# Second step of a two-layer graph kernel: norm statistics of four rows in two groups, and the top-eight pass between reading the flags and loading their register

## Chip, cores and metric

The kernel runs on one core of a Trainium2 chip. The metric is the device time of one launch in microseconds (us), lower is better: the median of three runs before the change is 4236.88 us (4235.11 to 4237.03).

## What is computed

Layer 0 is a graph attention over 4096 nodes with a dense 0/1 adjacency, residual and layer norm. Layer 1, cut to what matters here, is

```
for n in range(2):
    A  = top_p(softmax((Xa@W1.T@W2.T) @ (Xa@W3.T).T), 0.9)   # 4096 x 4096, rows renormalised
    Xf = R @ Xf                                               # R = (adj + I) / row sums
    Xa = A @ Xa
    Z  = Z + Xf @ U1[n].T + Xa @ U2[n].T
h = layernorm(X + Z) * ln_g + ln_b
out = layernorm(X + h)
```

`top_p` keeps, in each row, the smallest set of largest probabilities whose sum reaches 0.9. The layer norm is `(h - mean) / sqrt(var + 1e-5)`.

## The kernel before

The five engines run programs written out by hand and meet only through semaphores. Layer 0 comes first, then two steps `s = 0` and `s = 1` of layer 1. The change is in the second step (`s == 1`), which begins near 2400 us. It works through 32 tiles n of 128 rows each, with a score row of 4096 per partition, in three score buffers.

**VectorE**, per tile t: `search(t)` waits for the exponentials (`xp`) and for three halvings that ScalarE has already made (`lt`), makes three full passes over the scores (L1265), calls `final_stats(t)`, makes a fourth full pass (L1271), takes the top eight of 16 chunks (L1277), and sorts 48 candidates (L1284, L1286). `threshold(t)` (L1297 to L1325) works out the cut in some twenty small instructions and signals `lv`. `finish(t)` marks ties (L1333, L1334), calls `rmax(t + 2)`, waits for the row of flags that TensorE has turned (`pl`), reduces it to one integer (L1381), loads that integer into a register (L1382), branches on it (L1383; the branch's body is hardly ever run), and writes the masked scores (L1392), which signals `mask`. `rmax(t)` is one top-eight pass over 4096 scores (L1212) and a negation of the largest (L1213), which signals `mx`. In this code `link(ins)` lets the engine's next instruction wait until `ins` has completed.

`final_stats(n)` makes the mean and variance of rows of 128 x 256 for the two closing layer norms. Slots of two row tiles each enter the pipe from tile n = 17 on (`fslot`). For each of up to four row tiles (two that wait for `f1`, two that wait for `fa`) `stats_of` runs four instructions: `bn_stats` (L1232), `bn_aggr` (L1233), the negated mean (L1234) and variance plus epsilon (L1235), then signals `s2` or `s1`. Three of the four are linked. It is called with two row tiles at n = 18, with four at n = 19 to 31, and after the last tile in the loop's own extra rounds n = 32 to 36.

**GpSimd**, per round n: `r_post` (L529 to L537) ends the rows of R, `final_second`, `final_first` and `final_add` do the norms of three different slots (`norm` is L543 to L545), `scale_a` (L509 to L515) and `accumulate` (L523) end a tile of A @ Xa, and `bracket(n + 2)` (L484 to L503) prepares the search of tile n + 2. It starts when ScalarE signals `e8`, and its L492 signals `bt`.

**ScalarE**, per round n: evicts the turned scores, the logits of tile n + 3 (L958) and small products, runs three halvings of tile n + 1 (L1012 waits for `bt`; L1013, L1014 are full passes), evicts row 2p of R (L1043), runs `expo(n + 2)` (L994 waits for `mx`, L1002 ends with `e8`) and evicts row 2p + 1.

**TensorE**, per round n: `Tr(n - 1)` (L804) waits for `mask`, then logits (L760), small products, `AV(n - 1)` (L815), `Rmul(2p)` (L719), `gather_level(n)` (L821, waits for `lv`), `Rmul(2p + 1)` (L719). Rows r = 2p of R run up to 64: 32 for the first product, then 32 for the second, which reads `y_d` back into SBUF at n = 15.

**SyncE** loads the adjacency chunks, and stores and reloads `y_d`, `h_d`, `z_d` and `out`, in one queue in program order.

Of the kernel before, what the change touches and what calls it, by code (L numbers as in the profile page):

```python
# [9 lines left out]
ALU = mybir.AluOpType  # L10
# [7 lines left out]
EPS = 1e-5  # L18
# [8 lines left out]
def gat_topp_kernel(nc, xT, x, adj, adjTb, Wp, WT, aT, res_w, bias, res_b, ident, sel,  # L27
                    W1, W2T, W3T, U1T, U2T, ln_g, ln_b, out):
    N = adj.shape[0]
    NT = N // 128  # L30
# [19 lines left out]
    fslot = {max(HT + m - RLEAD + 2, 2 * m + 4): m for m in range(HT)}  # L50
# [10 lines left out]
    with ctx:  # L61
# [18 lines left out]
        def bank(b, n=1):  # L80
            return ps[:, 512 * b:512 * (b + n)]

        def sem(name):
            return ctx.enter_context(nc.semaphore(name))
# [70 lines left out]
        e8 = r1.take(8)  # L155
# [8 lines left out]
        m8 = r1.take(2, 8)  # L164
# [24 lines left out]
        fin = r1.take(6, 256)  # L189
        finx = r1.take(4, 256)  # L190
        finz = r1.take(2, 256)
        lns = r1.take(4, 16)
# [13 lines left out]
        def scores(s, t):  # L206
            return eb[:, t % (2 + s), 0:N]
# [70 lines left out]
        for s in range(2):  # L278
            g = {}
            for n in ("kt", "kc", "km", "kk", "pl", "el", "mx", "xp", "mask", "av", "R", "rv", "pz", "gx",  # L280
                      "gd", "po", "rd", "xs", "acc", "nz", "hi", "gi", "yd", "ys", "fi", "fa", "s1", "f1", "s2",
                      "fo", "fd", "lv", "lr", "lt", "qd", "e8", "bt", "bf", "xc"):
                g[n] = sem(f"{n}_{s}")
            g["aj"] = [sem(f"aj{i}_{s}") for i in range(AJR)]
            g["xd"] = [sem(f"xd{i}_{s}") for i in range(2)]
            st.append(g)
# [158 lines left out]
        def _(po):  # L445
# [13 lines left out]
            for i in range(16):  # L459
                last = nc.gpsimd.memset(iota[:, i:i + 1], float(i))  # L460
# [4 lines left out]
            def plink(ins):  # L465
                pc[0] += 1
                ins.then_inc(s_pc, 1)
                po.wait_ge(s_pc, pc[0])

            tt = nc.gpsimd.tensor_tensor  # L470
            ts = nc.gpsimd.tensor_scalar
            for s in range(2):
                g = st[s]
# [66 lines left out]
                def norm(r, dst, sem_):  # L540
                    a = lns[:, r % 4, :]
                    po.wait_ge(sem_, r + 1)
                    plink(tt(a[:, 8:9], a[:, 6:7], mhalf, ALU.pow))  # L543
                    plink(tt(a[:, 9:10], a[:, 8:9], a[:, 7:8], ALU.mult))
                    return ts(dst, fin[:, r % 6, :], a[:, 8:9], a[:, 9:10], ALU.mult, ALU.add)  # L545

                def final_add(m):
                    po.wait_ge(g["fi"], 16 * 6 * (m + 1))
# [4 lines left out]
                def final_first(m):  # L553
                    for r in (2 * m, 2 * m + 1):
                        f = fin[:, r % 6, :]
                        plink(norm(r, f, g["s1"]))
                        plink(tt(f, f, gb[:, 0, :], ALU.mult))
                        plink(tt(f, f, gb[:, 1, :], ALU.add))
                        tt(f, f, finx[:, r % 4, :], ALU.add).then_inc(g["f1"], 1)

                def final_second(m):
                    for r in (2 * m, 2 * m + 1):
                        norm(r, fin[:, r % 6, :], g["s2"]).then_inc(g["fo"], 1)
# [547 lines left out]
        def _(ve):  # L1111
            v = nc.vector

            def link(ins):
                dvc[0] += 1
                ins.then_inc(s_dv, 1)
                ve.wait_ge(s_dv, dvc[0])

            def done(sm_):
                ve.sem_inc(sm_, 1)  # L1120
# [7 lines left out]
            dst = WA[:, :, 256:264].rearrange("p k (h e) -> p k h e", e=2)[:, :, :, 1]  # L1128
            v.tensor_copy(WD[:, :, 0:4], dst)
            last = v.tensor_copy(WD[:, :, 32:36], dst)  # L1130
# [69 lines left out]
            def inner(ins):  # L1200
                ins.then_inc(s_br, 1)
                ve.wait_ge(s_br, 1)
                ve.sem_clear(s_br)

            for s in range(2):
                g = st[s]
                theta, mid, G, tmp, hi, ghi, t_, c8, r_, nt_, lo, nota, x_, y_ = (sm[:, 2 + i:3 + i] for i in range(14))
                cut, part, rl, rr = (sm[:, 16 + i:17 + i] for i in range(4))

                def rmax(t):  # L1210
                    ve.wait_ge(g["el"], eat[t])
                    link(v.max(m8[:, t % 2, :], scores(s, t)))  # L1212
                    v.tensor_scalar(sm[:, t % 2:t % 2 + 1], m8[:, t % 2, 0:1], -1.0, None,  # L1213
                                    ALU.mult).then_inc(g["mx"], 1)

                def cmax(t):
                    E = scores(s, t)
                    CK = N // NCHUNK[0]
                    for c in range(NL // 2):
                        ve.wait_ge(g["el"], eat[t] - NL // 2 + 1 + c)  # L1220
                        for lo_ in (c * 512, N // 2 + c * 512):
                            for k in range(lo_ // CK, (lo_ + 512) // CK):
                                last = v.max(cand[:, t % 2, k * 8:k * 8 + 8], E[:, k * CK:(k + 1) * CK])
                    link(last)
                    top = cand[:, t % 2, :].rearrange("p (c e) -> p c e", e=8)[:, :, 0]
                    link(v.tensor_reduce(m8[:, t % 2, 0:1], top, AX.X, ALU.max))
                    v.tensor_scalar(sm[:, t % 2:t % 2 + 1], m8[:, t % 2, 0:1], -1.0, None,
                                    ALU.mult).then_inc(g["mx"], 1)

                def stats_of(r, sem_):  # L1230
                    a = lns[:, r % 4, :]
                    link(v.bn_stats(a[:, 0:6], fin[:, r % 6, :]))  # L1232
                    link(v.bn_aggr(a[:, 10:12], a[:, 0:6]))  # L1233
                    v.tensor_scalar(a[:, 7:8], a[:, 10:11], -1.0, None, ALU.mult)  # L1234
                    link(v.tensor_scalar(a[:, 6:7], a[:, 11:12], EPS, None, ALU.add))  # L1235
                    done(sem_)

                def final_stats(n):
                    if s == 1 and n - 2 in fslot:
                        for r in (2 * fslot[n - 2], 2 * fslot[n - 2] + 1):  # L1240
                            ve.wait_ge(g["f1"], r + 1)
                            stats_of(r, g["s2"])
                    if s == 1 and n - 1 in fslot:
                        for r in (2 * fslot[n - 1], 2 * fslot[n - 1] + 1):
                            ve.wait_ge(g["fa"], r + 1)
                            stats_of(r, g["s1"])

                def search(t):
                    E = scores(s, t)
# [77 lines left out]
                def mark(sync, t, j):  # L1327
                    io = iota[:, 8 * j:8 * j + 8]
                    v.tensor_scalar(w8[:, 0, :], io, rl, t_, ALU.is_lt, ALU.mult)
                    sync(v.tensor_scalar(w8[:, 1, :], io, rr, t_, ALU.is_lt, ALU.mult))  # L1330
                    src = scores(s, t) if j == 0 else V
                    HN = N // 2
                    v.match_replace(out=V[:, 0:HN], in_to_replace=w8[:, 0, :], in_values=src[:, 0:HN], imm_value=2.0)  # L1333
                    sync(v.match_replace(out=V[:, HN:N], in_to_replace=w8[:, 1, :], in_values=src[:, HN:N],  # L1334
                                         imm_value=2.0))
# [32 lines left out]
                def finish(t):  # L1368
                    E = scores(s, t)
                    VN = V[:, 0:N]  # L1370
                    if s == 1:
                        mark(link, t, 0)
                        if t + 2 < NT:
                            rmax(t + 2)
                    if s == 0:
                        ve.wait_ge(g["lr"], t + 1)
                        flags = levr[0:1, :]
                    else:
                        ve.wait_ge(g["pl"], levat[t])
                        flags = bank(2 * ((levat[t] - 1) % 3))[0:1, 0:128]  # L1380
                    link(v.tensor_reduce(levi[0:1, :], flags, AX.X, ALU.max))  # L1381
                    level = ve.value_load(levi[0:1, :], min_val=0, max_val=2)  # L1382
                    with ve.If(level >= 1):  # L1383
                        if s == 0:
                            mark(inner, t, 0)
                        mark(inner, t, 1)
                        with ve.If(level >= 2):
                            exact(E)
                        if s == 0:
                            inner(v.scalar_tensor_tensor(out=E, in0=VN, scalar=t_, in1=E, op0=ALU.is_gt,  # L1390
                                                         op1=ALU.mult))
                    v.scalar_tensor_tensor(out=E, in0=VN if s else E, scalar=cut if s else t_, in1=E,  # L1392
                                           op0=ALU.is_gt if s else ALU.is_ge, op1=ALU.mult).then_inc(g["mask"], 1)
# [17 lines left out]
                if s == 0:  # L1411
                    cmax(0)
                else:
                    rmax(0)
# [50 lines left out]
```

## Time and profile before

| | |
|---|---|
| median of 3 runs | 4236.88 us |
| profiled execution, its own time | 4236.94 us |
| its span | 4235.1 us |
| PE busy | 3719.9 us (88%) |
| DVE busy | 3636.8 us (86%) |
| ACT busy | 3106.2 us (73%) |
| POOL busy | 1198.8 us (28%) |
| chain that ended last | PE 53%, DVE 19%, ACT 13%, issue 12% |

PE is TensorE, DVE VectorE, ACT ScalarE, POOL GpSimd, SP SyncE. Busy shares are averages over the whole launch; the chain is a share of the span. The idle time in front of an instruction is put down to what released it. The profiled execution's own time is 1.8 us longer than its span, and 0.06 us above the median.

### The profile page before, as it was taken

What the parts mean: (1) busy time and instruction counts of PE and PEld (TensorE: products, weight loads), DVE (VectorE), ACT (ScalarE), POOL (GpSimd) and SP (SyncE); (2) the same over time, 40 slices, a digit from 0 to 9 for tenths busy, and PEclk for the clock granted to TensorE, in tenths of its full rate; (3) what the DMA queues carried; (4) which work ended last, traced back from release to release, by engine and by line L of the source; (5) the groups of instructions that cost most, each with busy time, mean ns of one, the idle gap of its engine ahead of it and who ended that gap; (6) DMA issues with size and microseconds to landing.
All of it is one profiled execution on the core that took longest, in us unless ns stands there. A gap on an engine that the chain in (4) does not pass through costs nothing.

```text
span 4235.1 us, 66160 instructions
## 1 busy us (share of the span) xinstructions
PE 3719.9 (88%) x25300; PEld 3123.6 (74%) x25300; DVE 3636.8 (86%) x6431; ACT 3106.2 (73%) x3129; POOL 1198.8 (28%) x1444
## 2 busy tenths in 40 slices
PE   8677777777877777999999988999999999999984
PEld 5677777777777765777777757888888888777774
DVE  2899999999999957888888459999999899999995
ACT  3788988989899865555555348888788788777771
POOL 0000000000000000001000135555555567777774
PEclk8899999999999988999999989999999999999997
DMA  3211111111111120000000122333333333333331
GB/s 115 99 46 48 66 46 59 55 48 66 46 51 63 48 71 11 16 16 16 20 16 16 58 71 78 102 102 100 100 99 99 123 113 111 107 105 105 105 101 44
DMA packets 131757, 292.47 MB, mean 69 GB/s; under 512 B 14122, under 2 KB 94186, under 8 KB 127058
## 3 DMA queue, kind: packets, MB, share of 16 engines
q1 hardware_dynamic: 131410, 287.99, 21.3%
q8 instruction: 200, 3.28, 0.3%
q14 instruction: 147, 1.20, 0.1%
HBM read 250.19 MB, written 37.75 MB: 68 GB/s over the span
## 4 chain that ended last, share of the span: by engine, by line
PE 53%; DVE 19%; ACT 13%; issue 12%; POOL 1%; DMA 1%; DVEq 0%; SPq 0%; POOLq 0%; ACTq 0%
PE ps L815 16%; PE ps L719 11%; PE ps L658 9%; ACT b L894 7%; DVE b L1265 5%; PE ps L804 4%; PE ps L760 4%; ACT b L888 3%; PE ps L639 2%; DVE b L1277 2%; DVE b L1271 2%; DVE b L1212 2%; ACT b L882 1%; PE ps L792 1%; PE ps L782 1%
## 5 line engine op out<-in xcount | busy, mean ns | idle before, releaser
L719 PE MATMUL ps<-b 128*128 128x257 f32 x4096 | 913.0, 382 | 7.2 <-DMA b<-y_d 4.4
L815 PE MATMUL ps<-b 128*128 128x257 f32 x4096 | 901.2, 379 | 0.0
L658 PE MATMUL ps<-cb,b 128*128 128x128 f32 x4096 | 608.0, 312 | 322.0 <-ACT b L888 322.0
L719 PEld LDWEIGHTS ps<-b 128*128 128x128 f32 x4096 | 775.8, 191 | 132.9 <-issue 16.1
L815 PEld LDWEIGHTS ps<-b 128*128 128x128 f32 x4096 | 770.8, 189 | 111.4
L658 PEld LDWEIGHTS ps<-cb,b 128*128 128x128 f32 x4096 | 547.4, 163 | 371.4 <-ACT b L888 329.5
L1177 DVE SCALAR_TENSOR_TENSOR b<-b 128x4096 f32<-128x4096 f32 x128 | 566.5, 4426 | 62.1 <-ACT b L882 58.7
L1179 DVE CUSTOM_DVE_ANT_0 b<-b 128x4096 f32<-128x4096 f32 x128 | 566.4, 4425 | 5.9 <-DMA b<-in_adj 1.5
L894 ACT ACTIVATE b<-ps 128x1024 f32<-128x1024 f32 x512 | 499.9, 1022 | 75.1 <-PE ps L658 73.7
L639 PE MATMUL ps<-b 128*64 128x128 f32 x8192 | 503.6, 276 | 0.0
L888 ACT ACTIVATE b<-b 128x4096 f32<-128x4096 f32 x128 | 474.4, 3706 | 8.4 <-DVE b L1181 8.4
L639 PEld LDWEIGHTS ps<-b 128*64 128x64 f32 x8192 | 442.0, 137 | 42.9 <-issue 39.1
L453 POOL TENSOR_TENSOR cb<-cb 128x1 f32<-128x1 f32 x32 | 39.4, 1230 | 1519.7 <-DVE cb L1163 1519.7
L1265 DVE SCALAR_TENSOR_TENSOR b<-b 128x4096 f32<-128x4096 f32 x99 | 444.0, 4485 | 3.5
L1013 ACT ACTIVATE b<-b 128x4096 fp8e4<-128x4096 f32 x93 | 345.0, 3709 | 7.8 <-ACT kr L975 5.4
L1014 ACT ACTIVATE b<-b 128x4096 fp8e4<-128x4096 f32 x93 | 344.9, 3709 | 3.0
L1392 DVE SCALAR_TENSOR_TENSOR b<-b 128x4096 f32<-128x4096 f32 x64 | 287.0, 4485 | 67.3 <-issue 41.8
L882 ACT ACTIVATE b<-b 128x2560 f32<-128x2560 f32 x128 | 310.4, 2425 | 2.3 <-SPq L224 2.3
L994 ACT ACTIVATE b<-b 128x4096 f32<-128x4096 f32 x64 | 237.1, 3704 | 94.7 <-DVE b L1213 91.2
L1090 ACT ACTIVATE b<-ps 128x1024 f32<-128x1024 f32 x256 | 242.5, 1031 | 67.8 <-PE ps L804 67.4
L804 PEld LDWEIGHTS ps<-cb,b 128*128 128x128 f32 x2048 | 233.5, 143 | 69.1 <-DVE b L1392 51.4
L804 PE MATMUL ps<-cb,b 128*128 128x128 f32 x2048 | 241.7, 278 | 45.7 <-DVE b L1392 45.7
(188 smaller groups left out, 4880.3 us busy)
## 6 DMA issues: line engine op xcount, KB each, us to landing
b<-in_adjTb SPq DMA_DIRECT2D x256, 512.0 KB, 3.8
b<-in_adj SPq DMA_DIRECT2D x32, 2048.0 KB, 8.3
y_d<-b SPq DMA_DIRECT2D x64, 128.0 KB, 2.3
h_d<-b SPq DMA_DIRECT2D x64, 128.0 KB, 2.3
b<-h_d SPq DMA_DIRECT2D x64, 128.0 KB, 3.2
b<-in_xT SPq DMA_DIRECT2D x1, 4096.0 KB, 14.9
b<-in_x SPq DMA_DIRECT2D x32, 128.0 KB, 2.2
b<-y_d SPq DMA_DIRECT2D x32, 128.0 KB, 2.1
```

The costliest lines, as they stand in the source:

```text
L639: last = mm(bank(6 + t % 2)[half, 128 * h:128 * h + 128], h_s[:, j, 64 * h:64 * h + 64], pt[:, gq % PTR, b, :], start=(j < 2), stop=(j >= ...
L658: last = nc.tensor.transpose(bank(2 * (gq % 3), 2)[:, b * 128:(b + 1) * 128], ub[:, u % UB, j * 128:(j + 1) * 128], ident_s)
L719: last = mm(b[:, 0:XA], aj[:, q % AJR, e, :], xf[:, j, :], start=(j == 0), stop=(j == NT - 1))
L804: last = nc.tensor.transpose(o[:, b * 128:(b + 1) * 128], scores(s, t)[:, j * 128:(j + 1) * 128], ident_s)
L815: last = mm(o[:, 0:XA], at[:, q % ATR, b, :], xa[:, j, :], start=(j == 0), stop=(j == NT - 1))
L882: act(ub[:, u % UB, LSP:N], sd_s[:, h, LSP:N], ACT.Identity, bias=ssc[:, t, 2 * h:2 * h + 1]).then_inc(s_e, 1)
L888: act(b, b, ACT.Exp, bias=nm[:, u:u + 1], accum_out=zp[:, u:u + 1]).then_inc(s_x, 1)
L894: act(pt[:, gq % PTR].rearrange("p a b -> p (a b)"), bank(2 * (gq % 3), 2)[:, 0:CW], ACT.Copy).then_inc(s_ev, 1)
L1013: alink(act(junk, e, ACT.Sign, bias=neg, accum_out=C, saturate=False))
L1177: link(v.scalar_tensor_tensor(out=b, in0=b, scalar=SLOPE, in1=b, op0=ALU.mult, op1=ALU.max))
L1179: link(v.tensor_tensor_reduce(out=b, in0=b, in1=adj_s[:, t % 2, :], scale=1.0, scalar=-3.0e38, op0=ALU.mult, op1=ALU.max, accum_out=nm[:, ...
L1265: link(v.scalar_tensor_tensor(out=VN, in0=E, scalar=mid, in1=E, op0=ALU.is_gt, op1=ALU.mult, accum_out=G))
```

## The change

Three edits, all in the second step.

- `final_stats` gathers its row tiles first: all `bn_stats` one after the other, one link, then all `bn_aggr`, each of which signals its row itself. The negated mean and the variance plus epsilon leave VectorE.
- `norm` on GpSimd adds epsilon itself, one linked instruction more, and subtracts the product of mean and scale where it added the product with the negated mean.
- `rmax` is cut into `rtop` (the top-eight pass) and `rneg` (the negation). In `finish` of the second step `rtop(t + 2)` is issued behind the reduction of the flags and ahead of the register load, `rneg(t + 2)` behind the load and ahead of the branch. A new semaphore `tp` takes the place of the link between the two.

```diff
@@ norm (GpSimd)
                     po.wait_ge(sem_, r + 1)
+                    plink(ts(a[:, 6:7], a[:, 11:12], EPS, None, ALU.add))
                     plink(tt(a[:, 8:9], a[:, 6:7], mhalf, ALU.pow))
-                    plink(tt(a[:, 9:10], a[:, 8:9], a[:, 7:8], ALU.mult))
-                    return ts(dst, fin[:, r % 6, :], a[:, 8:9], a[:, 9:10], ALU.mult, ALU.add)
+                    plink(tt(a[:, 9:10], a[:, 8:9], a[:, 10:11], ALU.mult))
+                    return ts(dst, fin[:, r % 6, :], a[:, 8:9], a[:, 9:10], ALU.mult, ALU.subtract)
@@ rmax (VectorE)
-                def rmax(t):
+                def rtop(t):
                     ve.wait_ge(g["el"], eat[t])
-                    link(v.max(m8[:, t % 2, :], scores(s, t)))
+                    v.max(m8[:, t % 2, :], scores(s, t)).then_inc(g["tp"], 1)
+
+                def rneg(t):
+                    ve.wait_ge(g["tp"], t + 1)
                     v.tensor_scalar(sm[:, t % 2:t % 2 + 1], m8[:, t % 2, 0:1], -1.0, None,
                                     ALU.mult).then_inc(g["mx"], 1)
@@ final_stats (VectorE)
-                def stats_of(r, sem_):
-                    a = lns[:, r % 4, :]
-                    link(v.bn_stats(a[:, 0:6], fin[:, r % 6, :]))
-                    link(v.bn_aggr(a[:, 10:12], a[:, 0:6]))
-                    v.tensor_scalar(a[:, 7:8], a[:, 10:11], -1.0, None, ALU.mult)
-                    link(v.tensor_scalar(a[:, 6:7], a[:, 11:12], EPS, None, ALU.add))
-                    done(sem_)
...
+                    for r, ready, seen in rows:
+                        ve.wait_ge(ready, r + 1)
+                        last = v.bn_stats(lns[:, r % 4, 0:6], fin[:, r % 6, :])
+                    if rows:
+                        link(last)
+                    for r, ready, seen in rows:
+                        v.bn_aggr(lns[:, r % 4, 10:12], lns[:, r % 4, 0:6]).then_inc(seen, 1)
@@ finish (VectorE)
                     if s == 1:
                         mark(link, t, 0)
-                        if t + 2 < NT:
-                            rmax(t + 2)
...
                     link(v.tensor_reduce(levi[0:1, :], flags, AX.X, ALU.max))
+                    ahead = s == 1 and t + 2 < NT
+                    if ahead:
+                        rtop(t + 2)
                     level = ve.value_load(levi[0:1, :], min_val=0, max_val=2)
+                    if ahead:
+                        rneg(t + 2)
                     with ve.If(level >= 1):
```

VectorE's instructions at the flags of one tile of the second step, before (b is SBUF, ps is PSUM):

```order
L1333 MATCH_REPLACE b<-b 128x2048 [waits s_dv]
L1334 MATCH_REPLACE b<-b 128x2048
L1212 MAX b<-b 128x8 [waits el_1,s_dv]
L1213 TENSOR_SCALAR b<-b 128x1 [waits s_dv]
L1381 TENSOR_REDUCE b<-ps 1x1 [waits pl_1]
L1382 TENSOR_LOAD b [waits s_dv]
L1382 ISA x2
L1383 COMPARE_AND_BRANCH
```

and the same place in the change:

```order
L1336 MATCH_REPLACE b<-b 128x2048 [waits s_dv]
L1337 MATCH_REPLACE b<-b 128x2048
L1382 TENSOR_REDUCE b<-ps 1x1 [waits pl_1,s_dv]
L1213 MAX b<-b 128x8 [waits el_1,s_dv]
L1386 TENSOR_LOAD b
L1386 ISA x2
L1217 TENSOR_SCALAR b<-b 128x1 [waits tp_1]
L1389 COMPARE_AND_BRANCH
```

The wait for the flags (`pl_1`) now stands ahead of the top-eight pass, and the load no longer carries a wait of its own: the one for the reduction (`s_dv`) is in front of the pass.

VectorE at `final_stats` of one such tile, two of its four row tiles, before:

```order
L1232 BN_STATS b<-b 128x6 [waits s_dv,fa_1]
L1233 BN_AGGR b<-b 128x2 [waits s_dv]
L1234 TENSOR_SCALAR b<-b 128x1 [waits s_dv]
L1235 TENSOR_SCALAR b<-b 128x1
L1232 BN_STATS b<-b 128x6 [waits s_dv,fa_1]
L1233 BN_AGGR b<-b 128x2 [waits s_dv]
L1234 TENSOR_SCALAR b<-b 128x1 [waits s_dv]
L1235 TENSOR_SCALAR b<-b 128x1
L1271 SCALAR_TENSOR_TENSOR b<-b 128x4096 [waits s_dv]
```

and all four row tiles in the change:

```order
L1245 BN_STATS b<-b 128x6 [waits f1_1,s_dv]
L1245 BN_STATS b<-b 128x6 [waits f1_1]
L1245 BN_STATS b<-b 128x6 [waits fa_1] x2
L1249 BN_AGGR b<-b 128x2 [waits s_dv]
L1249 BN_AGGR b<-b 128x2 x3
```

Sixteen instructions have become eight, and the waits on VectorE's own results (`s_dv`) two.

## Rows read from the trace of the kernel before

**Rows 1.** Busy time by stretch: PE, PEld, DVE, ACT, POOL, granted clock, DMA share, GB/s
```profile
2556.00:3423.00 867.00, 862.19 (x4246) 720.56 (x4246) 791.38 (x1393) 712.02 (x808) 485.95 (x490) 0.99 0.33 100
```

**Rows 2.** Waits of VectorE, 2556 to 3423 us: total, times, longest
```profile
DVE b L1381 <- PE ps L821: 33.4, 13, 9.9
```

**Rows 3.** Waits of TensorE, 3580 to 4183 us
```profile
PE ps L821 <- DVE b L1325: 33.8, 11, 13.2
PE ps L804 <- DVE b L1392: 25.1, 10, 10.4
```

**Rows 4.** TensorE in order of time, around flags of tiles 10, 11: start, us, line
```profile
3056.46 0.38 PE L821 MATMUL ps<-cb,b 128*1 128x128 f32 x2
3070.79 3.65 PE L804 MATMUL ps<-cb,b 128*128 128x128 f32 x32
...
3107.74 0.38 PE L821 MATMUL ps<-cb,b 128*1 128x128 f32 x2
```

**Rows 5.** VectorE in order of time, tile 10
```profile
3056.88 0.28 DVE L1381 TENSOR_REDUCE b<-ps 1x1 int32<-1x128 f32 x1 [1.72 <-PE ps L821]
3058.34 4.49 DVE L1392 SCALAR_TENSOR_TENSOR b<-b 128x4096 f32<-128x4096 f32 x1 [1.18 <-issue]
...
3063.11 4.48 DVE L1265 SCALAR_TENSOR_TENSOR b<-b 128x4096 f32<-128x4096 f32 x1
```

**Rows 6.** VectorE in order of time, flags of tile 25
```profile
3854.65 4.43 DVE L1212 MAX8 b<-b 128x8 f32<-128x4096 f32 x1
3859.12 0.15 DVE L1213 TENSOR_SCALAR b<-b 128x1 f32<-128x1 f32 x1
3859.19 0.27 DVE L1381 TENSOR_REDUCE b<-ps 1x1 int32<-1x128 f32 x1
3860.34 4.49 DVE L1392 SCALAR_TENSOR_TENSOR b<-b 128x4096 f32<-128x4096 f32 x1 [0.89 <-DVE b L1381]
```

**Rows 7.** Sources L1382, L1383, VectorE's sequencer: duration ns min/median/max
```profile
L1382 DVEq TENSOR_LOAD <-b x64: 302/304/543, 1633.1 to 4177.0; - x64
L1383 DVEq COMPARE_BRANCH  x64: 56/63/76, 1634.0 to 4177.6; - x64
```

**Rows 8.** VectorE in order of time, statistics of tile 26 (three more such groups follow)
```profile
3880.42 0.43 DVE L1232 BATCH_NORM_STATS2 b<-b 128x6 f32<-128x256 f32 x1
3880.88 0.18 DVE L1233 BATCH_NORM_AGGREGATE b<-b 128x2 f32<-128x6 f32 x1
3881.10 0.15 DVE L1234 TENSOR_SCALAR b<-b 128x1 f32<-128x1 f32 x1
3881.17 0.14 DVE L1235 TENSOR_SCALAR b<-b 128x1 f32<-128x1 f32 x1
...
3884.58 5.04 DVE L1271 SCALAR_TENSOR_TENSOR b<-b 128x4096 f32<-128x4096 f32 x1
```

**Rows 9.** VectorE by line, 3423 to 4183 us: count, busy us, mean ns, idle before
```profile
L1277 DVE MAX8 b<-b 128x8 f32<-128x256 f32 x224 | 74.6, 413 | 0.5
...
L1392 DVE SCALAR_TENSOR_TENSOR b<-b 128x4096 f32<-128x4096 f32 x15 | 67.3, 4485 | 15.4 <-issue 8.3 <-DVE b L1381 7.0
```

**Rows 10.** VectorE in order of time: tile 17's flags, tile 31's mask
```profile
3423.43 0.28 DVE L1381 TENSOR_REDUCE b<-ps 1x1 int32<-1x128 f32 x1 [2.37 <-PE ps L821]
...
4178.17 4.49 DVE L1392 SCALAR_TENSOR_TENSOR b<-b 128x4096 f32<-128x4096 f32 x1 [1.19 <-issue]
```

**Rows 11.** GpSimd in order of time, bracket of tile 12
```profile
3064.42 3.27 POOL L484 TENSOR_SCALAR b<-b 128x1 f32<-128x1 f32 x1 [14.06 <-ACTq L1003]
3067.76 0.19 POOL L485 TENSOR_SCALAR b<-b 128x1 f32<-128x1 f32 x1
...
3068.22 4.54 POOL L487 TENSOR_SCALAR b<-b 128x1 f32<-128x1 f32 x1
```

**Rows 12.** TensorE in order of time, tile 15: the reload of y_d
```profile
3303.41 17.12 PE L719 MATMUL ps<-b 128*128 128x257 f32 x64 [4.43 <-DMA b<-y_d]
```

**Rows 13.** VectorE in order of time, tail: statistics of the last row tile
```profile
4229.99 0.43 DVE L1232 BATCH_NORM_STATS2 b<-b 128x6 f32<-128x256 f32 x1 [2.96 <-POOL b L559]
```

More of the change, by code:

```diff
@@ L281, in gat_topp_kernel @@
                       "gd", "po", "rd", "xs", "acc", "nz", "hi", "gi", "yd", "ys", "fi", "fa", "s1", "f1", "s2",
-                      "fo", "fd", "lv", "lr", "lt", "qd", "e8", "bt", "bf", "xc"):
+                      "fo", "fd", "lv", "lr", "lt", "qd", "e8", "bt", "bf", "xc", "tp"):
                 g[n] = sem(f"{n}_{s}")
@@ L1208, in _, with rmax @@
                 cut, part, rl, rr = (sm[:, 16 + i:17 + i] for i in range(4))
-                def rmax(t):
+                def rtop(t):
                     ve.wait_ge(g["el"], eat[t])
-                    link(v.max(m8[:, t % 2, :], scores(s, t)))
+                    v.max(m8[:, t % 2, :], scores(s, t)).then_inc(g["tp"], 1)
+                def rneg(t):
+                    ve.wait_ge(g["tp"], t + 1)
                     v.tensor_scalar(sm[:, t % 2:t % 2 + 1], m8[:, t % 2, 0:1], -1.0, None,
                                     ALU.mult).then_inc(g["mx"], 1)
+                def rmax(t):
+                    rtop(t)
+                    rneg(t)
                 def cmax(t):
@@ L1228, in cmax @@
                                     ALU.mult).then_inc(g["mx"], 1)
-                def stats_of(r, sem_):
-                    a = lns[:, r % 4, :]
-                    link(v.bn_stats(a[:, 0:6], fin[:, r % 6, :]))
-                    link(v.bn_aggr(a[:, 10:12], a[:, 0:6]))
-                    v.tensor_scalar(a[:, 7:8], a[:, 10:11], -1.0, None, ALU.mult)
-                    link(v.tensor_scalar(a[:, 6:7], a[:, 11:12], EPS, None, ALU.add))
-                    done(sem_)
-                def final_stats(n):
[L1239 to L1246, printed above, removed]
+                def final_stats(n):
+                    rows = []
+                    for back, ready, seen in ((2, "f1", "s2"), (1, "fa", "s1")):
+                        if s == 1 and n - back in fslot:
+                            rows += [(2 * fslot[n - back] + i, g[ready], g[seen]) for i in range(2)]
+                    for r, ready, seen in rows:
[5 more added lines that the diff above has]
+                        v.bn_aggr(lns[:, r % 4, 10:12], lns[:, r % 4, 0:6]).then_inc(seen, 1)
                 def search(t):
```

## The prediction

> **What bounds the kernel now.** I read four views in this order: the busy times by stretch, the waits of TensorE and of VectorE, the two engines' instructions in order of time, and VectorE's groups by line. All edits lie in the second step, and it falls into two parts.
>
> From 2556 to 3423 us TensorE is busy for 862 of 867 us, VectorE for 791 [rows 1], and the idle time of VectorE is in front of the reduction of the flags, which TensorE delivers late: 33.4 us in 13 waits [rows 2]. From one flag product to the next TensorE needs 51.28 us (3056.46 to 3107.74) [rows 4]. This part is **TensorE's**: saving VectorE time there buys nothing.
>
> From 3580 to 4183 us it is the other way round. TensorE waits for `lv` (33.8 us) and for the mask (25.1 us) [rows 3], since `final_stats` has joined VectorE's work. VectorE waits for no other engine from the flags of tile 17, 3423.43, to the mask of tile 31, 4178.17 [rows 10]; from the reduction of tile 17 to that of tile 25, 3859.19, are 435.8 us [rows 6, 10], 54.5 a tile, and 54.7 without tile 18, which has half the statistics. In front of its masks it has 15.4 us of idle in 15 tiles, 1.03 each [rows 9]. This part is **VectorE's**: what is saved there shortens the launch, down to TensorE's 51.28 a tile, which leaves 3.4 us a tile to be had.
>
> **The statistics.** Before, a row tile takes 1.03 to 1.04 us from one `bn_stats` to the next: 0.46 to `bn_aggr`, 0.22 to L1234, 0.07 to L1235, the rest behind the link [rows 8]; four of them fill 4.16 us, 3880.42 to 3884.58. The change leaves four `bn_stats`, one link, four `bn_aggr`. How close do instructions with no wait between them stand? L1235 starts 0.07 behind a 0.15 us instruction [rows 8], and 224 top-eight instructions of 413 ns mean fill 74.6 us, 333 ns each [rows 9]: both overlap by 0.08. So the four `bn_stats` take 3 x 0.35 + 0.43 = 1.48, the link 0.03, the four `bn_aggr` 3 x 0.10 + 0.18 = 0.48, and the fourth pass starts 0.08 before the end: 1.92 us. The saving is 2.24 us for four row tiles and, in the same way, 1.05 for the two of tile 18. Tiles 19 to 31 are 13: 13 x 2.24 + 1.05 = **30.2 us**. If nothing overlaps, four row tiles take 4 x 0.46 + 4 x 0.22 = 2.72 and the saving is 1.44 each; with `bn_aggr` at 0.07 it is 2.33. I take 2.24, as both neighbours in the trace overlap.
>
> A rule speaks against this. The Trainium skill, page "VectorE: DVE Perf Modes", section "The DRAIN you can't avoid", says that chaining VectorE instructions without semaphores saves nothing: eight copies took the same time either way. This trace shows 0.07 us from start to start for a 0.15 us instruction and does not agree; by the rule the saving would be the 1.44 of the lower end.
>
> **The register load.** Before, it stands bare between reduction and mask. In tile 25 the reduction starts at 3859.19 and the mask at 3860.34, with 0.89 us idle [rows 6]; in it lie the load of 0.30 and the branch of 0.06 us [rows 7], and register work. Tiles vary between 0.9 and 1.2. In the change the load stands behind a top-eight pass of 4.43 us, so it and the register work are covered, if the sequencer goes on while the pass runs. What stays is the branch and the issue of the mask, some 0.13 us of idle behind the negation, so 1.03 - 0.13 = 0.90 is saved. Against it go 0.16: the reduction overlapped the negation before (3859.12 and 3859.19) and is now followed by a link. That makes 0.74 a tile in tiles 18 to 29, 12 x 0.74 = **8.9 us**. Tiles 30 and 31 have no pass to hide behind and keep their load. No row shows a load beside a running pass: the ends are 0 and 1.0 us a tile, and I take 0.74 because the load reads one integer that has been finished and carries no wait any more.
>
> **The pass behind the flags.** In the first part VectorE used to run the pass while it waited for the flags; now it stands behind them. From reduction to mask was 1.46 us in tile 10 [rows 5] and will be 0.28 + 0.04 + 4.43 + 0.04 + 0.29 = 5.08: each mask comes 3.6 us later. Its end was 3062.83 [rows 5], and TensorE turned it only at 3070.79 [rows 4], so 8.0 us of slack become 4.4, and the cost is nothing there. The work hidden behind is the second row of R on TensorE. Queued behind the later pass are `mx`, ScalarE's exponentials, `e8` and GpSimd's `bracket`; the next who need these, the halvings of the next tile, have VectorE's whole search to come. Once, at the border of tile 17, the chain that VectorE then carries contains this pass and did not before: **+3.6 us**, and +0.4 because the flags of tile 18 come a little after its marks.
>
> **One place where later costs.** `r_post(15)`, behind `bracket(16)` in GpSimd's queue, makes the last rows of `y_d`; SyncE stores and reloads them, and TensorE waits 4.43 us for the reload [rows 12]. A GpSimd instruction that starts during a full VectorE pass ends with it: L484 started at 3064.42 and ended at 3067.69, the pass at 3067.59, and L487 took 4.54 us against 0.19 for L485 [rows 5, 11]. So `bracket` runs in step with VectorE's passes and shifts with them by 3.6 us, unless L484 slips in ahead of the first pass; then `bracket` gains one pass and `r_post` ends about 1.1 us earlier. By my arithmetic `e8` comes within 0.1 us of that pass's start. I take **+3.6**, with -1.1 as the other end.
>
> **GpSimd's extra instruction.** 64 in all, about 0.3 us each from start to start (L485 takes 0.19 [rows 11]). In full tiles GpSimd idles 14.06 us at a time [rows 11], and its results are due a round later: nothing. In the tail the two engines take turns and VectorE waits 2.96 us for GpSimd [rows 13]. There, two of them stand ahead of the last `accumulate` (+0.6), the first signal waits for the second row tile (+0.4, plus 0.3 for epsilon), the second row +0.3, and the last pair +1.4: together **+3.0 us**. No DMA is added; SyncE's queue changes only in when its waits end.
>
> **The start.** Tile 0's mask, for which TensorE waits, comes 0.6 us earlier: **-0.6**.
>
> Sum: -30.2 - 8.9 + 3.6 + 0.4 + 3.6 + 3.0 - 0.6 = **-29.1 us** against the profiled execution's 4236.94, so 4207.8; the median, 4236.88, is 0.06 lower, which changes nothing. Per tile the saving in the late part is 2.24 + 0.74 = 2.98, below the 3.4 at which TensorE takes over.
>
> **The rivals.**
> (a) The load waits for the pass in front of it. The saving of 8.9 is gone: 4216.7. For it: no row shows the contrary. In the profile the load would end behind the pass.
> (b) The instructions do not overlap, which is also the rule's case: 13 x 0.80 less, 4218.2. Against it: rows 8 and 9.
> (c) VectorE gains more than I count. Its fourth pass took 5.04 us beside GpSimd's `r_post` [rows 8], 4.49 elsewhere, and small instructions were stretched too. If shorter statistics move them apart, up to 0.4 a tile more counts before TensorE's 51.28 is reached, and the reload may fall to its other end: 4207.8 - 5 - 4.7 = 4198.
> (d) Slower than before: the exposed pass reaches TensorE. Place: the mask of tiles 4 to 16. Price: 3.6 us a tile and more, 13 x 3.6 = 47 us, so 4255. It decides from the point where the mask ends over 8.0 us later than now, 4.4 us beyond my shift; a late `lt` from ScalarE, behind a `bracket` that lost another pass of some 5 us, would do that. Against it: bracket's next pass is several us away.
> (e) The gain is lost again in the late part: `e8` comes behind the mask instead of ahead of it, `bracket` loses a pass, and ScalarE, late with its evictions, makes TensorE and so VectorE wait 1.9 us in each of 13 tiles: 4207.8 + 24.7 = 4232.5, about as before. For it: the negation, and all behind it, moves later against the mask. Against it: ScalarE is busy for 712 of 867 us even at TensorE's pace [rows 1].
>
> **The numbers.** 0.2%, 8.5 us, is about what a measurement can tell from no change. Forecast 0.50, (a) 0.12, (b) 0.11, (c) 0.13, (e) 0.08, (d) 0.06. Faster by over 8.5 us: forecast, a, b and c, 0.86; same: e, 0.08; slower: d, 0.06. The range leaves out d, e and the far ends of b and c: 4198 to 4219.
>
> **What would show it.** Right: about 1.9 us from the third halving's last instruction to the fourth pass, where it was 4.2; the load within the top-eight pass and about 0.15 us idle in front of the mask; flag waits in the first part unchanged near 2 us, masks there 3.6 us later against the flags; the late tiles at 51.3 to 52 us; the wait for `y_d` near 8 us; a tail about 3 us longer. Wrong: a mask wait of TensorE in tiles 4 to 16, waits of VectorE for `lt` or `xp`, late tiles still above 53.5 us, or a load behind the pass.

## The result and the profile after

The changed kernel takes 4208.43 us (median of four runs, 4207.35 to 4209.77), the kernel before 4235.99 (four runs). The ratio is 0.9935, 95% interval 0.9918 to 0.9952: 27.6 us faster. The forecast was 4207.8. The profiled execution took 4207.35 us at a span of 4205.6; that of before 4236.94 at 4235.1.

The sum is right to a microsecond, but two of its terms were off by five to six microseconds each, in opposite directions. Cut at the same events, the spans compare so:

| stretch | before | after | difference | forecast |
|---|---|---|---|---|
| start to the flags of tile 17 | 3423.4 | 3425.3 | +1.9 | +3.0 |
| to the end of tile 31's mask | 759.2 | 719.0 | -40.2 | -35.1 |
| tail | 52.4 | 61.2 | +8.8 | +3.0 |

Busy time by stretch, after: PE, PEld, DVE, ACT, POOL, granted clock, DMA share, GB/s.

```profile
2556.00:3425.00 869.00, 860.63 (x4244) 718.86 (x4242) 785.52 (x1388) 709.01 (x802) 501.86 (x490) 0.99 0.32 99
3425.00:4145.00 720.00, 697.15 (x3447) 584.76 (x3446) 683.50 (x1258) 556.41 (x634) 632.09 (x687) 0.99 0.36 109
4145.00:4206.00 61.00, 22.65 (x107) 19.70 (x105) 4.71 (x19) 5.91 (x9) 36.18 (x61) 0.67 0.10 33
```

TensorE is busy for 697 of 720 us in the late part. Its waits from 3500 us on are three, all at the last two tiles:

```profile
PE ps L805 <- DVE b L1398: 10.4, 1, 10.4
PE ps L770 <- POOL b L515: 9.0, 1, 9.0
PE ps L822 <- DVE b L1328: 3.4, 1, 3.4
```

Before, it waited 33.8 us for `lv` in 11 pieces and 25.1 us for the mask in 10 [rows 3]. VectorE, which waited for nobody there, now waits for the flags again:

```profile
DVE b L1382 <- PE ps L822: 13.6, 12, 2.9
DVE b L1398 <- issue: 4.7, 8, 1.2
```

The pace shows on TensorE, from the turning of one mask to the turning of the next. In order of time, with the first transposes of tiles 23 and 24 (the view ends at 3800, and the last row counts 18 of the 32):

```profile
3746.80 3.65 PE L805 MATMUL ps<-cb,b 128*128 128x128 f32 x32
...
3783.75 0.38 PE L822 MATMUL ps<-cb,b 128*1 128x128 f32 x2
3784.06 14.18 PE L720 MATMUL ps<-b 128*128 128x257 f32 x64
3798.08 2.13 PE L805 MATMUL ps<-cb,b 128*128 128x128 f32 x18
```

From 3746.80 to 3798.08 are 51.28 us, TensorE's own period of [rows 4] to the hundredth. The late part has become TensorE's, as far as the flags of tile 28: they are the last for which VectorE waits, 0.55 us.

VectorE after, first the flags of tile 29, then the statistics of tile 30, in order of time:

```profile
4037.53 2.28 DVE L1337 MATCH_REPLACE8 b<-b 128x2048 f32<-128x2048 f32 x1
4039.94 0.28 DVE L1382 TENSOR_REDUCE b<-ps 1x1 int32<-1x128 f32 x1
4040.25 4.43 DVE L1213 MAX8 b<-b 128x8 f32<-128x4096 f32 x1
4044.72 0.15 DVE L1217 TENSOR_SCALAR b<-b 128x1 f32<-128x1 f32 x1
4044.94 4.49 DVE L1398 SCALAR_TENSOR_TENSOR b<-b 128x4096 f32<-128x4096 f32 x1
```

```profile
4065.30 0.22 DVE L1271 SCALAR_TENSOR_TENSOR b<-b 128x1 f32<-128x1 f32 x1
4065.56 1.41 DVE L1245 BATCH_NORM_STATS2 b<-b 128x6 f32<-128x256 f32 x4
4067.00 0.38 DVE L1249 BATCH_NORM_AGGREGATE b<-b 128x2 f32<-128x6 f32 x4
4067.30 4.45 DVE L1274 SCALAR_TENSOR_TENSOR b<-b 128x4096 f32<-128x4096 f32 x1
```

Where [rows 6] had 0.89 us of idle in front of the mask there is now 0.07 (in some tiles 0.39). The register load of this tile, by its source line (start at the end of the row):

```profile
L1386 DVEq TENSOR_LOAD <-b x1: 307/307/307, 4040.3 to 4040.3; - x1
```

It starts with the top-eight pass at 4040.25 and is over 4 us before the pass is. The sequencer does run ahead. And the four row tiles of [rows 8], 4.16 us before, take 1.74 us, 4065.56 to 4067.30.

The small instructions at the end of `threshold` have become shorter too. In order of time, the two in front of the marks of tile 26, before:

```profile
3903.40 0.52 DVE L1329 TENSOR_SCALAR b<-b 128x8 f32<-128x8 f32 x1
3903.83 0.78 DVE L1330 TENSOR_SCALAR b<-b 128x8 f32<-128x8 f32 x1
```

and after:

```profile
3880.66 0.28 DVE L1332 TENSOR_SCALAR b<-b 128x8 f32<-128x8 f32 x1
3880.85 0.30 DVE L1333 TENSOR_SCALAR b<-b 128x8 f32<-128x8 f32 x1
```

From mask to mask, waits for the flags left out, VectorE needs 54.71 us before and 50.30 after (mean of tiles 19 to 28). Of the 4.41 us gained, 2.46 are the statistics, 0.45 the fourth pass, 1.06 the thresholds and the start of the marks, and 0.70 the stretch from the marks to the mask, where the load lies; the three passes ahead of the statistics have become 0.27 us longer.

### The profile page after: what moved, and what is told of

It reads as the page before. It is cut to its first block, busy times and chain, and to the rows that moved or that the text cites. A ratio compares the mean times of both kernels' runs of the same rounds, so it can differ in the third digit from the quotient of the medians.

```text
span 4205.6 us, 66062 instructions
## 1 busy us (share of the span) xinstructions
PE 3713.8 (88%) x25300; PEld 3122.7 (74%) x25300; DVE 3600.1 (86%) x6303; ACT 3108.2 (74%) x3129; POOL 1321.8 (31%) x1508
## 4 chain that ended last, share of the span: by engine, by line
PE 52%; ACT 25%; issue 11%; POOL 6%; DVE 4%; DMA 1%; SPq 0%; ACTq 0%; POOLq 0%; DVEq 0%
PE ps L816 16%; PE ps L720 10%; PE ps L659 9%; ACT b L895 7%; ACT b L1014 4%; ACT b L1015 4%; PE ps L805 4%; PE ps L761 4%; ACT b L889 3%; PE ps L640 3%; POOL b L490 2%; POOL b L487 2%; ACT b L995 2%; ACT b L883 1%; POOL b L484 1%
## 5 line engine op out<-in xcount | busy, mean ns | idle before, releaser
L889 ACT ACTIVATE b<-b 128x4096 f32<-128x4096 f32 x128 | 474.4, 3706 | 8.1 <-DVE b L1182 8.1
L1231 DVE MAX8 b<-b 128x8 f32<-128x128 f32 x1024 | 201.1, 278 | 80.2 <-ACT b L959 80.2
```

The costliest lines, as they stand in the source:

```text
L889: act(b, b, ACT.Exp, bias=nm[:, u:u + 1], accum_out=zp[:, u:u + 1]).then_inc(s_x, 1)
```

## Experiments

All were timed in five rounds beside the kernel before, which measured 4236.70 in the first group of four and 4236.94 in the second, 0.7 and 1.0 us more than beside the change.

### 1. The statistics alone

GpSimd's new norm stays in as well; the top-eight pass stands ahead of the flags as before.

```diff
                         mark(link, t, 0)
+                        if t + 2 < NT:
+                            rmax(t + 2)
...
-                    ahead = s == 1 and t + 2 < NT
+                    ahead = False
```

> The change with the top-eight pass left ahead of the flags, as before; the grouped statistics and GpSimd's norm stay. Theory A (the late part is TensorE's after the change, so its 51.3 us a tile is the floor): grouping alone saves 2.4 us a tile of VectorE's own work plus up to 1.5 us if the collisions with GpSimd go with it, so tiles 19 to 29 come near 51.3 to 52 us; no 3.6 us at the reload of y_d (its wait stays near 4.4 us), tail as in the change: about 4206 us, within 4 of the changed kernel. Rival B (the collisions of VectorE with GpSimd go only because the later pass pushes GpSimd's bracket behind the mask): the fourth pass still begins 0.5 us slower and the marks 0.7, tiles 52.3 us, about 4214.

Measured: 4201.65 us (4199.48 to 4202.74), ratio 0.9918 [0.9905, 0.9932]. That is 6.8 us **faster than the change**, where I had expected it within 4: the pass behind the flags costs time. In the profiled executions the difference is 7.0: 1.9 up to the flags of tile 17, 3.3 from there to the last mask, and 1.8 in the tail, where both kernels have the same program. 1.5 of these are TensorE turning the last mask, 5.19 us here and 6.66 there, which took 5.93 to 6.46 in the other profiled kernels with the new statistics, in either order; so nothing shows that this part belongs to the order of the pass. The late tiles run at 51.3 us here too. Rival B falls: the marks take 5.04 to 5.22 us (5.77 before in most tiles, from the `lv` instruction of `threshold` to the end of the second half), and the fourth pass is followed by the chunks after 4.69 us (4.7 to 5.3 before). So the collisions go without the later pass. At the fourth pass the shorter statistics are enough, in either form of the norm (4.69 in experiment 7 too); at the marks GpSimd's slower norm has a share, since with the multiply-add form (experiment 4) most marks take 5.34 to 5.54.

What became of them stands in GpSimd's groups by line (busy us, mean ns). The kernel before, 3423 to 4236 us:

```profile
L530 POOL TENSOR_TENSOR b<-b,cb 128x1 f32<-128x1 f32 x28 | 60.3, 2153 | 2.2
...
L498 POOL TENSOR_TENSOR b<-b 128x12 f32<-128x12 f32 x13 | 30.0, 2304 | 1.1
```

and with the statistics alone, 3423 to 4199 us:

```profile
L498 POOL TENSOR_TENSOR b<-b 128x12 f32<-128x12 f32 x13 | 81.4, 6260 | 1.1
...
L530 POOL TENSOR_TENSOR b<-b,cb 128x1 f32<-128x1 f32 x28 | 19.8, 706 | 2.2
```

Before, `bracket` was done when the fourth pass began; `r_post` got its first 256 elements in, and the pass was held up, then held `r_post` up in turn (L530). Now the pass begins 2.4 us earlier, catches `bracket` in L498, and `r_post` comes behind it (L530 at 706 ns mean in place of 2153). GpSimd pays with 4 us a tile in L498, which it has.

### 2. The pass behind the flags alone

The kernel before with the third edit only (`rtop`, load, `rneg`; statistics and norm as before).

> The kernel before with the third edit alone (pass behind the flags, load behind the pass), statistics and norm as before. Theory A: 0.74 us a tile in tiles 18 to 29 (8.9 us), 1.5 at the start, against 3.6 at the reload of y_d and 3.6 at tile 17: about 4232 to 4236, no clear difference. Rival B (later e8 takes away the collisions of VectorE with GpSimd): 1 to 1.5 us more a tile, 13 tiles, about 4218 to 4222.

Measured: 4237.96 us (4236.89 to 4240.19, eleven runs), ratio 1.0004 [0.9995, 1.0013]: no difference; theory A's range ended at 4236. The hidden load is real where VectorE is the bound. VectorE's waits from 3425 to 4184 us contain, in front of the mask,

```profile
DVE b L1402 <- issue: 3.9, 8, 1.2
DVE b L1402 <- DVE b L1386: 0.9, 1, 0.9
```

against 15.4 us of idle there before [rows 9]. From the flags of tile 17 to the last mask it takes 756.6 us in place of 759.2: 2.6 saved, after the exposed pass of tile 17 has been paid. Its late tiles (19 to 28) take 54.22 us in place of 54.71: 0.61 is gained between marks and mask and 0.38 at the fourth pass, and 0.51 is lost in the thresholds and the start of the marks. The first part costs more than that: the flags of tile 17 come 3.0 us later, and from those of tile 14 to those of tile 15, where `y_d` is reloaded, it takes 62.5 us in place of 58.9.

### 3. A link behind every statistics instruction

```diff
-                        last = v.bn_stats(lns[:, r % 4, 0:6], fin[:, r % 6, :])
-                    if rows:
-                        link(last)
+                        link(v.bn_stats(lns[:, r % 4, 0:6], fin[:, r % 6, :]))
...
-                        v.bn_aggr(...).then_inc(seen, 1)
+                        link(v.bn_aggr(...))
+                        done(seen)
```

> The change with a link behind every bn_stats and every bn_aggr. Theory A (instructions without a wait overlap by about 0.08 us): the four row tiles take 2.7 us in place of 1.78. Rival (VectorE drains behind every instruction anyway): 1.78 stays. In time: tiles 19 to 29 have about 1 us of waiting for the flags each, which covers most of it: 0 to 3 us more than the change, 4208 to 4212; if VectorE were still the bound, 0.9 x 13 = 12 us more, 4220.

Measured: 4216.52 us (4215.97 to 4217.54), 8.1 more than the change. In order of time, the same instructions as above:

```profile
3866.16 1.82 DVE L1245 BATCH_NORM_STATS2 b<-b 128x6 f32<-128x256 f32 x4
3868.02 1.17 DVE L1247 BATCH_NORM_AGGREGATE b<-b 128x2 f32<-128x6 f32 x4
3869.33 4.48 DVE L1273 SCALAR_TENSOR_TENSOR b<-b 128x4096 f32<-128x4096 f32 x1
```

3.17 us in place of 1.74. The four `bn_stats` lose 0.41, the four `bn_aggr` 0.79; these have an instruction of their own for the signal here too, and what that costs beside the link was not run by itself. The rule weighed in the prediction (Trainium skill, "VectorE: DVE Perf Modes", "The DRAIN you can't avoid"), that leaving the semaphores out between VectorE instructions saves nothing, does not hold for these instructions: it is worth 1.4 us for eight of them, and the measurement decides. The same section also says that a next instruction that is not held starts earlier, which the early starts in this trace bear out and which the prediction left out. The time went up by more than I expected, because the 1.4 us used up all of VectorE's 1 us of waiting, and the tiles take 51.5 to 52.4 us.

### 4. GpSimd's norm as multiply and add

GpSimd's groups by line in the changed kernel, 3425 to 4206 us, held a surprise:

```profile
L546 POOL TENSOR_SCALAR b<-b 128x256 f32<-128x256 f32 x64 | 79.1, 1235 | 6.8
```

The same instruction on the same 256 elements, with `add` in place of `subtract`, was L545 before:

```profile
L545 POOL TENSOR_SCALAR b<-b 128x256 f32<-128x256 f32 x64 | 36.1, 565 | 6.8
```

```diff
-                    plink(tt(a[:, 9:10], a[:, 8:9], a[:, 10:11], ALU.mult))
-                    return ts(dst, fin[:, r % 6, :], a[:, 8:9], a[:, 9:10], ALU.mult, ALU.subtract)
+                    plink(ts(a[:, 9:10], a[:, 8:9], a[:, 10:11], -1.0, ALU.mult, ALU.mult))
+                    return ts(dst, fin[:, r % 6, :], a[:, 8:9], a[:, 9:10], ALU.mult, ALU.add)
```

> The change with GpSimd's norm in the form multiply-add again: the product of mean and scale is negated by a tensor_scalar with -1. L546 took 1.24 us with subtract, L545 0.56 with add before. Theory A (subtract as the second operation costs GpSimd 0.68 us each, six of them one after another in the tail): L546 back at 0.56, tail shorter by 4 us, 4204. Rival (the 1.24 us come from something else, as the operand from another column, or the negation costs as much): no difference, 4208.

Measured: 4205.05 us (4204.38 to 4206.3), 3.4 less than the change. The last norm of the launch in this kernel:

```profile
4199.55 0.57 POOL L544 TENSOR_TENSOR b<-b,cb 128x1 f32<-128x1 f32 x1
4200.22 0.27 POOL L545 TENSOR_SCALAR b<-b 128x1 f32<-128x1 f32 x1
4200.59 0.55 POOL L546 TENSOR_SCALAR b<-b 128x256 f32<-128x256 f32 x1
```

and in the changed kernel:

```profile
4201.15 0.57 POOL L544 TENSOR_TENSOR b<-b,cb 128x1 f32<-128x1 f32 x1
4201.80 0.19 POOL L545 TENSOR_TENSOR b<-b 128x1 f32<-128x1 f32 x1
4202.09 1.23 POOL L546 TENSOR_SCALAR b<-b 128x256 f32<-128x256 f32 x1
```

The subtraction costs 0.68 us each; the product with -1 takes 0.27 us where the product without it took 0.19, so a norm is 0.5 us shorter in all. The tail, 61.2 us in the change, is 57.4 here.

### 5. Tile 14 alone in the old order

The pass stands ahead of the flags in tile 14 and behind them in all others.

> The change with tile 14 alone in the old order (its top-eight pass ahead of the flags). Theory A (the later pass of tile 14 delays e8, bracket(16) and with it r_post(15), y_d and its reload by 3.6 us): the wait for the flags of tile 15 falls from 14.3 back to about 9.9 us, the flags of tile 17 come 3.6 us earlier, about 4205 us. Rival B (each of tiles 0 to 14 adds its share, or the reload depends on something else in the change): less than 1 us of it comes back, 4208.

Measured: 4206.08 us (4204.71 to 4208.73), 2.3 less than the change; the two sets of runs overlap. The wait of tile 15 did not fall: 14.3 us. But it is the wrong gauge, since it counts from VectorE's arrival, and VectorE arrives earlier when its pass has been done. TensorE's own wait for the second product is the right one. Before it was 4.43 us [rows 12]; the changed kernel and then this experiment have:

```profile
3305.55 16.81 PE L720 MATMUL ps<-b 128*128 128x257 f32 x64 [8.37 <-ACTq L1038]
```

```profile
3305.28 12.68 PE L724 MATMUL ps<-b 128*128 128x257 f32 x48 [6.27 <-ACTq L1042]
```

So 2.1 of the 3.9 us come back. The chain is as stated, but one tile is not enough: tile 14 still starts from the late position that tile 13 left VectorE in, and ends its marks and its pass only after TensorE's flags. The profile puts the release down to ScalarE in the two later kernels, but in all three (before, change, this one) SyncE issues the reload 3.8 to 3.9 us ahead of TensorE's start (3299.53 to 3303.41, 3301.61 to 3305.55 and 3301.37 to 3305.28 us). I take the reload for the cause, without having taken it away.

### 6. Tiles 28 and 29 in the old order

> The change with tiles 28 and 29 in the old order. Theory A (the late part is TensorE's until the flags of tile 29; there the chain goes over to VectorE, and the pass behind those flags is exposed once): the mask of tile 29 comes 3.6 us earlier against its flags, the end 3 to 3.6 us earlier, about 4205. Rival B (VectorE carries the chain from tile 17 on, as the prediction had it): two tiles lose the hidden load, 1.5 us later, 4210.

Measured: 4207.83 us (4207.17 to 4209.5), as the change. Neither theory. VectorE's reductions of tiles 27 and 28, here and then in experiment 1:

```profile
3938.17 0.28 DVE L1388 TENSOR_REDUCE b<-ps 1x1 int32<-1x128 f32 x1 [0.67 <-PE ps L826]
...
3993.07 0.27 DVE L1388 TENSOR_REDUCE b<-ps 1x1 int32<-1x128 f32 x1
```

```profile
3936.12 0.28 DVE L1384 TENSOR_REDUCE b<-ps 1x1 int32<-1x128 f32 x1
...
3987.39 0.28 DVE L1384 TENSOR_REDUCE b<-ps 1x1 int32<-1x128 f32 x1 [0.25 <-PE ps L822]
```

Here 54.9 us lie between the two, in experiment 1 and in the change 51.3. From the reduction of tile 28 to the end of the last mask it takes 151.9 us here, 151.8 in experiment 1 and 155.0 in the change. So the change pays for a pass behind the flags of tile 28, and this kernel pays for it in front of them, where VectorE has only the 0.55 us that it waited. Experiment 1 pays neither: its VectorE has the pass done ahead of the flags in every tile from 17 on and is no later. That lead has to be kept from tile to tile; VectorE gains at most the 0.6 to 1.3 us a tile that it waits in tiles 18 to 28, and so can't get it back in two.

### 7. and 8. What the runs point to

Grouped statistics, the pass ahead of the flags in every tile, the multiply-add form, and behind the last tile each row tile's statistics signalled by itself:

```diff
                         last = v.bn_stats(lns[:, r % 4, 0:6], fin[:, r % 6, :])
+                        if n >= NT:
+                            link(last)
+                            v.bn_aggr(lns[:, r % 4, 10:12], lns[:, r % 4, 0:6]).then_inc(seen, 1)
+                    if n >= NT:
+                        return
```

> Grouped statistics, the pass ahead of the flags in all tiles, GpSimd's norm as multiply-add with a negated product, and in the rounds behind the last tile each row tile's statistics signalled by itself as before. If the gains of e1 (6.8 us against the change), e4 (3.4 us) and the tail (1 to 1.5 us) add up: 4197. If ScalarE and GpSimd (bt, lt) set the pace of the late tiles now, the tail alone gains: 4199.

Measured: 4196.35 us (4195.8 to 4196.91), ratio 0.9904 [0.9889, 0.9919]: 40.6 us faster than before, 12.1 faster than the change. The gains add up.

With the pass behind the flags in tile 0 and tiles 18 to 27:

> As e7_best, but the pass behind the flags in tile 0 and tiles 18 to 27. If a hidden load is worth anything where TensorE and VectorE are level: 0.6 to 1.5 us at tile 0 and up to 0.7 in a few late tiles, 4195 to 4196. If the later e8 costs more there than the load gives: equal to e7_best or up to 3 us above it.

Measured: 4200.77 us (4198.63 to 4202.29), 4.4 more, outside both forecasts. Where the order changes, the lead of a pass is given away; VectorE at tile 18, in order of time:

```profile
3476.26 0.28 DVE L1393 TENSOR_REDUCE b<-ps 1x1 int32<-1x128 f32 x1 [4.38 <-PE ps L826]
3476.57 4.43 DVE L1217 MAX8 b<-b 128x8 f32<-128x4096 f32 x1
3481.04 0.15 DVE L1221 TENSOR_SCALAR b<-b 128x1 f32<-128x1 f32 x1
3481.58 4.48 DVE L1409 SCALAR_TENSOR_TENSOR b<-b 128x4096 f32<-128x4096 f32 x1 [0.39 <-issue]
```

4.38 us of waiting for the flags, and behind them a pass that would have all but fitted into it. The flags still come every 51.3 us up to tile 27; the price shows where the old order returns, 55.2 us from the reduction of tile 27 to that of tile 28. From the flags of tile 17 to the last mask this kernel takes 720.1 us, the seventh 716.7. The profiled execution is 2.6 us behind the seventh's already at the flags of tile 17, with the mask of tile 0 4.0 us later; the pass of tile 0 alone doesn't explain it, as that mask ends at 2554.7 to 2557.0 in the other kernels with the pass there, and at 2555.4 in the seventh.

## Why the prediction was right, and where it was not

- **The bound.** Right: the early part was and stayed TensorE's. There the flags' waits of VectorE, 1.6 to 2.4 us before, are 2.5 to 3.2, where I had said unchanged: 4.43 us of pass have left the way to the flags, and the later mask puts back only part of it. The masks come 3.8 us later against the flags (3.6 forecast), and TensorE turns them without a wait.
- **The statistics.** The mechanism was right, the size a little low: 2.24 was forecast for four row tiles, and 1.74 us in place of 4.16 is 2.42. The four `bn_aggr` take 0.38, not 0.48. By experiment 3 the missing waits are worth 1.4 of it; the other 1.0 is that eight instructions are fewer than sixteen.
- **The register load.** Right in mechanism and size: 0.07 or 0.39 us of idle in place of 0.88 to 1.2, and 0.70 us a tile between marks and mask where 0.74 was forecast. But in the kernel as changed it is worth next to nothing, since the tiles run at TensorE's pace.
- **Who bounds the late part.** This step failed. I took the saving to be 2.98 us a tile, below the 3.4 at which TensorE takes over, and put the collisions with GpSimd at nothing in the sum and at 0.4 a tile in rival (c). The runs show 0.45 us less at the fourth pass and 1.06 in the thresholds and the start of the marks, against 0.27 more in the other passes. VectorE gained 4.4 us a tile; TensorE allowed 3.4. The stretch lost 40.2 us, not 35.1, and rival (c)'s mechanism was in fact at work.
- **The pass behind the flags.** The +3.6, once, at the border of tile 17, was right in size and wrong in place. With TensorE as the bound, the border lies where VectorE takes the chain over, behind the flags of tile 28: up to these the change and experiment 1 take the same 564.0 us from those of tile 17, and from there to the last mask 155.0 against 151.8. The price from the flags of tile 17 to the last mask is 719.0 against 715.8 us, and in experiment 8 720.1 against 716.7.
- **The reload of `y_d`.** +3.6 forecast; TensorE waits 8.37 us in place of 4.43, which is +3.9, and from the flags of tile 14 to those of tile 15 it is +3.6. Its main step, `bracket` moving with VectorE's passes, is borne out by GpSimd's times: `r_post(15)` ended 35.8 us behind the reduction of tile 14 before, and 39.6 after.
- **The start.** -0.6 forecast, -1.5 in the profiled execution. The two can't be told apart: the mask of tile 0 ends between 2554.7 and 2559.4 us in profiled executions of kernels whose program up to there is the same or nearly so.
- **The tail.** The second step that failed: +3.0 forecast, +8.8 measured. I counted GpSimd's instructions and not that one of them changed its second operation. Where two norms stand together, one takes 2.45 us from start to start in place of 1.45: 0.31 for the added instruction and 0.68 for the subtraction. Eight norms follow the last `scale_a`, and 1.8 us of what they add falls into the wait for `X`, 2.18 us in place of 3.98; experiment 4 gave back 3.8 of the tail. Another 1.0 us is TensorE turning the last mask more slowly, 6.66 us in place of 5.63, at a granted clock of 0.55 in place of 0.65 of full speed; it had idled 10.4 us ahead of that in both kernels. The other profiled kernels have between 5.19 and 6.46, so this part is not shown to come from the change.
- **The two errors.** -5.1 in the late part, +5.8 in the tail and -1.1 ahead of both nearly cancel; that the measured time lies so near 4207.8 is luck. The change as a whole is 27.6 us faster, but beside the new statistics its third edit is a loss of 6.8 (experiment 1; 5.2 of it in the stretches up to the last mask of the profiled executions), and its form of the norm one of 3.4 (experiment 4).

## What to carry to other kernels

An instruction that fills an engine's waiting time is free where it stands; moved behind the wait, it is paid wherever that engine carries the chain next, even if it now hides something smaller itself. When a change relieves one of two engines that are close to level, work out the other's period first, and count the small stretches by contention as part of what can be gained: here they were over a quarter of what VectorE gained. And an instruction with another operation in it is a new instruction, which needs its own price in each place where instructions of that engine stand one behind another.

## What the runs showed of the hardware

- GpSimd's `tensor_scalar` on 128 x 256 float32 takes 1.24 us with multiply and subtract, and 0.55 with multiply and add (the change and experiment 4, 64 instructions each).
- VectorE's sequencer carries out a register load of 0.31 us and its checks while a 4.43 us pass runs in front of it; what is left between a negation and the instruction behind the branch is 0.07 or 0.39 us, where it was 0.88 to 1.2 us with the load bare (profiles of the change and of before).
- Four `bn_stats` of 0.43 us without waits take 1.41 us, with a link behind each 1.82; four `bn_aggr` 0.38, and with a link and a signal of its own behind each 1.17 (the change and experiment 3).
